# A macaron block (FFN, gated delta-rule attention, FFN) on one core: a new order of the attention core's products, statistics and halves, and centring on TensorE

## What is computed

```python
x = x + 0.5 * ffn(layernorm(x))
x = x + attn(layernorm(x))
x = x + 0.5 * ffn(layernorm(x))        # the same weights as the first

def ffn(x):
    h = silu(x @ w1.T * w1_s) * (x @ w2.T * w2_s)     # 128 -> 512
    h = gelu(h @ h1.T * h1_s)                          # 512 -> 512, exact gelu
    h = gelu(h @ h2.T * h2_s)                          # 512 -> 512
    return h @ w3.T * w3_s                             # 512 -> 128

def attn(hs):                                          # 4 heads of 32
    q, k, v = (silu(dwconv4(hs @ W)) for W in (Wq, Wk, Wv))
    beta = sigmoid(hs @ Wb)
    o_d = delta_rule_chunkwise(q, k, v, beta)          # chunks of 32: T = inv(I + strict(kb k')), then a recurrence over 8 chunks
    paths = [fir3(v), fir15(v), fir64(v), o_d, v]      # five paths, 32 wide per head
    stats = mean, mean square, mean abs, norm of each path, each broadcast over 32 channels
    logits = gelu([hs, stats] @ gW1 + gb1) @ gW2 + gb2
    probs = softmax(logits / tau) * (1 - sum(eps)) + eps
    o = sum_p probs_p * paths_p
    return (o * rsqrt(mean(o*o) + 1e-5) * norm_w) @ Wo
```

## Time and profile before

| | |
|---|---|
| median of 3 runs | 507.91 us (507.79 to 508.33) |
| the profiled execution | 507.65 us |
| its span, first to last instruction | 505.9 us |
| TensorE / weight loads / VectorE / ScalarE / GpSimd busy | 397.9 / 293.3 / 314.0 / 290.1 / 9.9 us |
| mean granted TensorE clock | 0.858 |

### The profile page before, as it was taken

One profiled execution on the slowest core, in us unless ns is written; L12 is line 12 of the kernel. 1 busy time (PEld: TensorE's weight loads), 2 busy tenths in 40 slices (PEclk: granted clock), 3 DMA queues, 4 the chain that ended last, 5 costly groups with the idle time before them and its releaser, 6 DMA issues.

```text
span 505.9 us, 9754 instructions
## 1 busy us (share of the span) xinstructions
PE 397.9 (79%) x4162; PEld 293.3 (58%) x4162; DVE 314.0 (62%) x467; ACT 290.1 (57%) x415; POOL 9.9 (2%) x36
## 2 busy tenths in 40 slices
PE   5579999999889869779587816608673599989997
PEld 2446776678657559477477814303322448666785
DVE  2883579565037597999154774893358845676633
ACT  5866857895665754965326133211525448686973
POOL 3000000000000100000100000000000000000000
PEclk9779999999999956979957556858786979999999
DMA  8700008100000000024700000000000000001001
GB/s 280 246 1 1 3 1 264 29 3 0 2 0 0 2 3 3 0 64 128 224 12 6 4 1 1 0 1 0 0 0 1 1 1 1 1 2 43 3 1 41
DMA packets 13428, 17.38 MB, mean 34 GB/s; under 512 B 832, under 2 KB 9024, under 8 KB 13376
## 3 DMA queue, kind: packets, MB, share of 16 engines
q1 hardware_dynamic: 13232, 16.58, 10.6%
q10 hardware_dynamic: 144, 0.01, 0.0%
HBM read 15.55 MB, written 1.05 MB: 33 GB/s over the span
## 4 chain that ended last, share of the span: by engine, by line
PE 56%; DVE 20%; ACT 14%; issue 8%; DMA 2%; SPq 0%; DVEq 0%; ACTq 0%
PE ps_a L654 11%; PE ps_a L655 11%; PE ps_a L848 5%; PE ps_a L745 4%; PE ps_a L789 3%; ACT arena L569 3%; DVE arena L1123 2%; PE ps_d L811 2%; PE ps_a L801 2%; PE ps_a L811 2%; DVE acts L968 2%; PE ps_d L712 2%; PE ps_d L655 2%; PE ps_d L654 2%; PE ps_a L832 1%
## 5 line engine op out<-in xcount | busy, mean ns | idle before, releaser
L654 PE MATMUL ps_a<-acts,w_f 128*128 128x512 f32 x256 | 104.4, 408 | 1.3 <-DVE acts L968 1.0
L655 PE MATMUL ps_a<-acts,w_f 128*128 128x512 f32 x256 | 101.4, 396 | 0.0
L654 PEld LDWEIGHTS ps_a<-acts,w_f 128*128 128x128 f32 x256 | 49.2, 192 | 14.7 <-issue 1.4
L655 PEld LDWEIGHTS ps_a<-acts,w_f 128*128 128x128 f32 x256 | 49.1, 192 | 11.6 <-issue 1.4
L539 ACT ACTIVATE acts<-ps_a,vec 128x512 fp32r<-128x512 f32 x64 | 44.3, 692 | 0.0
L987 DVE TENSOR_TENSOR acts<-gbuf,acts 128x512 fp32r<-128x512 f32 x32 | 21.6, 688 | 32.7 <-ACT acts L539 32.7
L745 PE MATMUL ps_a<-xnp,conv_w 128*128 128x512 f32 x156 | 38.3, 403 | 0.0
L987 DVE TENSOR_TENSOR acts<-ghbuf,acts 128x512 fp32r<-128x512 f32 x32 | 21.4, 690 | 25.4 <-ACT acts L539 25.4
L745 PEld LDWEIGHTS ps_a<-xnp,conv_w 128*128 128x128 f32 x156 | 29.3, 188 | 8.3 <-issue 1.4
L848 PE MATMUL ps_a<-arena,ident 128*128 128x512 f32 x40 | 22.8, 737 | 13.4 <-DVE arena L1123 13.4
L823 PE MATMUL ps_d<-arena 32*32 32x64 f32 x448 | 13.8, 275 | 24.4 <-issue 14.7
(11 more groups left out here) (192 smaller groups left out, 810.5 us busy)
## 6 DMA issues: line engine op xcount, KB each, us to landing
toep<-in_fir SPq DMA_DIRECT2D x16, 288.0 KB, 5.1
w_in<-in_h SPq DMA_DIRECT2D x4, 1024.0 KB, 8.4
g_rows<-in_gW SPq DMA_DIRECT2D x4, 640.0 KB, 6.6
w_in<-in_w SPq DMA_DIRECT2D x6, 256.0 KB, 4.1
iobuf<-in_x SPq DMA_DIRECT2D x4, 256.0 KB, 6.6
toep<-in_taps SPq DMA_DIRECT2D x1, 768.0 KB, 6.8
y<-iobuf SPq DMA_DIRECT2D x3, 256.0 KB, 2.4
toep<-in_proj SPq DMA_DIRECT2D x1, 256.0 KB, 9.0
```

The source lines that it names most:

```text
L654: e.matmul(bank, w, hi, start=start, stop=False)
L655: return e.matmul(bank, w, lo, start=False, stop=stop)
```

## The change

Nothing of the arithmetic's meaning changes. What is done, part by part:

- Layer norm: a third constant matrix `cent_w`, identity minus 1/128, so that the product of "mean" is x already centred, in PSUM. ScalarE squares it from there; VectorE's subtraction goes, and `refine` reads the centred x from PSUM. The bank is held until `refine` has read it.
- First FFN: "scan" of h1 stands before "var", "scan" of h2 and w3 behind the means of tiles 2 and 3, "flag" of it behind their "var". "flag" uses ring A and its number is made by ScalarE. The rounding of h2 and w3 stands behind the first "hid1" on ScalarE.
- Tables of ScalarE's functions are loaded ahead by one-element operations (`preload`).
- "gram": ScalarE copies one half out of each bank, VectorE masks the other. The temperature numbers on ScalarE so come behind gram.
- The last four "fir" groups are interleaved with "yy" of half 0. All statistics of paths 0 to 2 and 4 (both halves) are split into single reductions ("r1", "r2", "r3") and squares ("sq") and stand before and between the steps of half 0's recurrence. Half 1's recurrence has gates, logits and softmax of half 0 between its steps. "bo" of half 1 comes behind that recurrence of half 0, "aq" between its steps.
- "logit" leaves PSUM through ScalarE, with bias and scale.
- "mix" is in quarters ("mul" 0 to 3, 16 of the 32 tokens of each row each). Quarter 0 is added by identity products, the other three by three VectorE adds each ("add"), with a square on ScalarE ("osq").
- Gates 2 and 3 and logits 2 and 3 move into the second FFN around the first "up"; what is left of half 1 is put between single blocks of "hid1" and "hid2" by the table `FILL`, on VectorE and ScalarE. "wo" 2 and 3 come behind "hid2" of tile 0; mean and variance of tiles 2 and 3 behind "hid2" of tile 1.

```diff
@@ ffn_steps
-    s += [("soft", 2, 1)] if last else []
-    s += [("var", f, 0)]
-    s += [] if last else [("flag", f, 0)]
-    s += [("var", f, 1)]
+    s += [] if last else [("flag", f, 0), ("scan", f, 1)]
+    s += [("var", f, 0), ("var", f, 1)]
...
-            s += [("scan", f, 1), ("up", f, a), ("flag", f, 1), ("scan", f, 2), ("up", f, b), ("flag", f, 2)]
+            s += [("up", f, a), ("flag", f, 1), ("up", f, b)]
         elif more:
-            s += [("up", f, a), ("mix", 2, 1), ("up", f, b), ("addmix", 2, 1)]
+            s += [("gate", 2, 2), ("gate", 2, 3), ("up", f, a), ("logit", 2, 2), ("logit", 2, 3), ("up", f, b)]
...
-            s += [("hid1", f, a), ("scale", 2, 1), ("hid1", f, b), ("wo", 2, 2), ("wo", 2, 3), ("hid2", f, a),
-                  ("mean", f, 2), ("mean", f, 3), ("var", f, 2), ("var", f, 3), ("hid2", f, b)]
+            s += [("hid1", f, a), ("hid1", f, b), ("hid2", f, a), ("wo", 2, 2), ("wo", 2, 3), ("hid2", f, b),
+                  ("mean", f, 2), ("mean", f, 3), ("var", f, 2), ("var", f, 3)]
         elif more:
             s += [("hid1", f, a), ("in", f, a + 2), ("in", f, b + 2), ("mean", f, a + 2), ("mean", f, b + 2),
-                  ("hid1", f, b), ("var", f, a + 2), ("var", f, b + 2), ("hid2", f, a), ("hid2", f, b)]
+                  ("scan", f, 2), ("hid1", f, b), ("var", f, a + 2), ("var", f, b + 2), ("flag", f, 2), ("hid2", f, a), ("hid2", f, b)]
@@ att_steps
-    s += [("fir", 2, i) for i in range(16)]
-    s += [("turn4", 2, 0), ("turn4", 2, 1)]
-    s += [("yy", 2, h) for h in range(4)] + [("aq", 2, b) for b in range(4)]
-    s += [("stat", 2, 0)] + [("bo", 2, b) for b in range(4)] + [("round", 2, 0)]
-    ahead = [(kind, 2, 4 + k) for kind in ("yy", "aq", "bo") for k in range(4)]
-    extra = {2: ("stat", 2, 1), 4: ("stat", 2, 2), 6: ("stat", 2, 3), 7: ("stat", 2, 4)}
+    s += [("fir", 2, i) for i in range(12)]
+    for k in range(4):
+        s += [("yy", 2, k), ("fir", 2, 12 + k)]
+    s += [("turn4", 2, 0), ("turn4", 2, 1), ("sq", 2, 0), ("sq", 2, 1)] + sums(0) + [("sq", 2, 2)] + sums(1)
+    s += [("sq", 2, 3), ("aq", 2, 0), ("r1", 2, 2), ("aq", 2, 1), ("r2", 2, 2), ("r3", 2, 2), ("sq", 2, 4),
+          ("aq", 2, 2), ("r1", 2, 3), ("aq", 2, 3), ("r2", 2, 3), ("r3", 2, 3)]
+    s += [("bo", 2, b) for b in range(4)] + [("sq", 2, 5)] + sums(4)
+    ahead = [("yy", 2, k) for k in range(4, 8)] + [("aq", 2, k) for k in range(4, 8)]
+    between = {1: [("r1", 2, 5)], 2: [("r2", 2, 5), ("r3", 2, 5), ("sq", 2, 6)], 3: [("numbers", 2, 0), ("r1", 2, 6)],
+               4: [("r2", 2, 6), ("r3", 2, 6), ("sq", 2, 7), ("round", 2, 0)], 5: [("r1", 2, 7)], 6: [("r2", 2, 7)],
+               7: [("r3", 2, 7)]}
     for n in range(1, NCH):
-        s += [("rec", 2, n)] + ahead[2 * n - 2:2 * n]
-        s += [extra[n]] if n in extra else []
-    s += [("turn3", 2, 0), ("stat", 2, 5), ("turn", 2, 0)]
...
+        s += [("rec", 2, n), ahead[n - 1]] + between[n]
+    s += [("aq", 2, 7), ("turn3", 2, 0), ("sq", 2, 8)] + [("bo", 2, b) for b in range(4, 8)] + sums(8) + [("turn", 2, 0)]
+    half = [("rec", 2, NCH + n) for n in range(1, NCH)]
+    s += [half[0], ("gate", 2, 0), half[1], ("gate", 2, 1), half[2], ("logit", 2, 0), half[3], ("logit", 2, 1), half[4],
+          ("lturn", 2, 0), half[5], ("soft", 2, 0), half[6], ("prob", 2, 0), ("mul", 2, 0), ("addmix", 2, 0),
+          ("mul", 2, 1), ("add", 2, 1), ("osq", 2, 1), ("turn3", 2, 1), ("sq", 2, 9), ("rms", 2, 0), ("r1", 2, 9),
+          ("scale", 2, 0), ("r2", 2, 9), ("r3", 2, 9), ("wo", 2, 0), ("wo", 2, 1), ("turn", 2, 1)]
...
+FILL = {("hid1", 0, 0): [("lturn", 1)], ("hid1", 0, 1): [("soft", 1)], ("hid1", 0, 2): [("prob", 1)],
+        ("hid1", 0, 3): [("mul", 2)], ("hid1", 1, 1): [("mul", 3)], ("hid1", 1, 3): [("add", 2), ("osq", 2)],
+        ("hid2", 0, 0): [("add", 3), ("osq", 3)], ("hid2", 0, 2): [("rms", 1)], ("hid2", 0, 3): [("scale", 1)]}
@@ ScalarE
+            def preload(table):
+                settle()
+                own(e.activation(vc("rt0"), vc("lneps"), table))
+            def late(kind, i):
+                if kind == "soft":
+                    e.wait_ge(S["dve_sub"], i + 1)
+                    e.activation(ex5[:, i], ex5[:, i], ACT.Exp).then_inc(S["act_exp"], 1)
+                    preload(ACT.Gelu if i else ACT.Abs_reciprocal_sqrt)
+                elif kind == "osq":
+                    r = slice(HB * (i % 2), HB * (i % 2) + HB)
+                    e.wait_ge(S["summed"], i if i else 1)
+                    e.activation(o_sq[:, r], paths[0][:, i // 2, r], ACT.Square).then_inc(S["act_osq"], 1)
+                elif kind == "rms":
+                    e.wait_ge(S["dve_ms"], i + 1)
+                    e.activation(rt, var, ACT.Abs_reciprocal_sqrt).then_inc(S["act_rms"], 1)
+                    preload(ACT.Gelu if i else ACT.Sqrt)
...
+                elif kind == "flag":
+                    e.wait_ge(S["pe_a"], a + 1)
+                    e.activation(low_any[:, i:i + 1], bank[:, 0:1], ACT.Copy, scale=128.0).then_inc(S["act_a"], 1)
+                elif kind == "gram":
+                    e.wait_ge(S["dve_nrm"], NT)
+                    for h in range(H):
+                        e.wait_ge(S["pe_d"], dd + h + 1)
+                        e.activation(alt[:, i, h, :, 0], ps_d[:, (dd + h) % NRING].rearrange(
+                            "p (n a t) -> p n a t", n=NCH, a=2)[:, :, 0], ACT.Copy).then_inc(S["act_l"], 1)
...
+                        for k, n in FILL.get((kind, i, m), ()) if f else ():
+                            late(k, n)
+                    if s == ("hid1", 0, 0):
+                        e.wait_ge(S["ld_hid"], 32)
+                        e.activation(w_f[0][:, 3072:5632], w_in[0][:, 3072:5632], ACT.Copy).then_inc(S["hid_round"], 1)
@@ TensorE
-                    e.wait_ge(S["dve_d"], D_AT[("flag", 0, n)] + 1)
+                    e.wait_ge(S["act_a"], A_AT[("flag", 0, n)] + 1)
...
-                    e.matmul(take_d(dd), mean_w[:, :], tile(x_t, i), start=True, stop=True
+                    e.matmul(take_d(dd), cent_w[:, :], tile(x_t, i), start=True, stop=True
@@ VectorE
-            def refine(bank, half_y2, y, src, eps, out, shape, free):
-                e.scalar_tensor_tensor(out=half_y2, in0=bank, scalar=eps, in1=half_y2, op0=ALU.add, op1=ALU.mult
-                                       ).then_inc(S["dve_d"], 1)
-                own(e.scalar_tensor_tensor(out=src, in0=src, scalar=-1.0, in1=y, op0=ALU.mult, op1=ALU.mult))
+            def refine(bank, half_y2, y, centred, src, eps, out, shape, done, freed):
+                own(e.scalar_tensor_tensor(out=half_y2, in0=bank, scalar=eps, in1=half_y2, op0=ALU.add, op1=ALU.mult))
+                e.scalar_tensor_tensor(out=src, in0=centred, scalar=-1.0, in1=y, op0=ALU.mult, op1=ALU.mult
+                                       ).then_inc(S["dve_d"], done)
...
+                elif kind == "mul":
+                    g, r = i // 2, slice(HB * (i % 2), HB * (i % 2) + HB)
+                    w = pr5[:, g, r].rearrange("p t c -> p c t").unsqueeze(3).to_broadcast([128, P, HB, DH])
...
+                elif kind == "add":
+                    g, r = i // 2, slice(HB * (i % 2), HB * (i % 2) + HB)
+                    settle()
+                    own(e.tensor_tensor(pall[:, 0:2, g, r], pall[:, 0:2, g, r], pall[:, 2:4, g, r], ALU.add))
+                    settle()
+                    own(e.tensor_tensor(paths[0][:, g, r], paths[0][:, g, r], paths[1][:, g, r], ALU.add))
+                    settle()
+                    e.tensor_tensor(paths[0][:, g, r], paths[0][:, g, r], paths[4][:, g, r], ALU.add
+                                    ).then_inc(S["summed"], 1)
```

More of the change, by code:

```diff
@@ L99 @@
-RING_D = {"mean": 1, "flag": 1, "var": 1, "up": KT, "down": 1, "sumsq": 2, "gram": H, "aq": 1, "rec": 1,
-          "logit": 1, "wo": 1}
+RING_A = {"in": 1, "flag": 1, "gsum": 1, "up": KT, "hid1": KT, "hid2": KT, "out": 1, "qkv": 4, "window": 1, "token": 1, "fir": 1,
+          "yy": 1, "bo": 1, "gate": 2, "logit": 1, "addmix": 1}
+RING_D = {"mean": 1, "var": 1, "up": KT, "down": 1, "sumsq": 2, "gram": H, "aq": 1, "rec": 1,
+          "wo": 1}
 def ring_of(step):
```

299 lines of the change are left out of this document (151 added, 148 removed).

## The result

The changed kernel takes 484.27 us (median of 4 runs, 483.71 to 485.25); the kernel before, run beside it, 507.85 (506.75 to 508.33). The ratio is 0.9541, 95% interval 0.9519 to 0.9563: 23.6 us faster. The forecast was 487.5, in a range of 473 to 500. The profiled execution of the changed kernel has a span of 483.5 in 485.25 us.

What follows compares the result with a forecast made beforehand. TensorE was busy 79% of the span, but the bound was taken to change from stage to stage. 507.65 us with +4.4 -0.25 -25.1 +0.8 = -20.2 gave 487.5; own range 480 to 494, 8 in 10 473 to 500.

Steps and rivals of the forecast that it cites:

- 1. First FFN: First FFN: removed waits give -8.2 us; rounding, the flag ahead of hid2 and clock falls turn it to +4.4.
- 2. Convolution to inverse: Convolution, gram, inverse: +0.3 us; centring spares 0.25, gram evacuation costs 0.5, the temperature numbers nothing at the end.
- 3. To the first state: Up to half 0's recurrence: +2.6 us including gram's 0.5; VectorE's queue moves the first state's transpose from 265.1 to 267.7.
- 4. Recurrences: Both halves' recurrences: -8.4 us at half 1's first state (VectorE 26.2 plus waits), then -32.8 at the output projection.
- 5. Second FFN's start: Softmax, multiply and addmix leave, gates and logits enter: hid1 at 363.3 instead of 416.1, -52.8 us there.
- 6. What is given back: Second FFN: half 1's work between hidden blocks gives back 27.7 us; TensorE waits 20 for "wo 2"; -25.1 is left.
- The pause looked for ahead of "out": Second FFN, a sign of being right: TensorE idle about 5 us before "out", followed by a granted clock of 0.5.
- The fillers don't fit: Rival, second FFN: fillers fit, TensorE finds wo 2 ready, 16 of the 20 us come back, 471; chance 0.10.
- The flag isn't free: Rival, first FFN: the flag costs nothing, hid1's pauses are covered, -8.2 stays instead of +4.4, 475; chance 0.15.
- The core gives: Rival, half 0: core doesn't give, instruction supply or slow clock bounds it, -8.4 and 3 more go, 499; chance 0.15.
- The clock doesn't stay low: Rival, hid2 of tile 1 to the end: clock stays low after the 20-us pause, up to 537; chance 0.05.

Runs made afterwards that it cites:

- flag_first: Changed kernel with the h2 flag moved ahead of the variances of tiles 2 and 3 in the first FFN: 478.78 us, ratio 0.9432.
- no_centre: Changed kernel with the mean product and VectorE's subtraction brought back, no centring on TensorE: 488.82 us, ratio 0.9646.
- numbers_first: Changed kernel with ScalarE's temperature numbers back in front of gram: 484.38 us, ratio 0.9528.
- short_abs: Changed kernel whose VectorE sums of absolute values read only 4 of the 32 channels of a head: 483.46 us, ratio 0.9513.
- wo_late_lag: Changed kernel with "wo" 2 and 3 behind hid2 of tile 1, and ScalarE's squares and root one or two gelus later: 475.56 us, ratio 0.9374.

## Why the prediction held, step by step

Positions before and after (us into the span), with the shift that the steps of the prediction give, sums of its steps, and the shift measured:

| position | before | after | forecast | measured |
|---|---|---|---|---|
| attention core starts | 124.14 | 127.91 | +4.4 | +3.8 |
| first state, half 0 | 265.12 | 269.59 | +6.8 | +4.5 |
| first state, half 1 | 306.49 | 300.74 | -4.3 | -5.8 |
| "wo 0" | 370.32 | 341.27 | -28.7 | -29.1 |
| hid1, second FFN | 416.06 | 365.71 | -48.7 | -50.4 |
| hid2 of tile 1 | 445.75 | 414.71 | -29.7 | -31.0 |
| first silu, tiles 2 and 3 | 460.70 | 438.31 | -21.0 | -22.4 |
| end of the span | 505.9 | 483.5 | -20.2 | -22.4 |

(Forecast shifts of the rows from half 0 on are the steps' figures plus 4.4 - 0.25.)

**1. First FFN.** Right in kind and near in size. hid1 starts at 26.94, 5.9 earlier (5.3 forecast), and its first tile runs at full clock, worth 2.9 as forecast. (Its instructions there are 32, not 64; the 7.3 us of the prediction fit 32.) The pause ahead of the means takes back 4.0 (2.9 forecast) and the fall of the clock behind it 1.9 (2.4): from 40.27 to the end of hid1 at 51.30 are 11.0 us, from 45.05 to 54.17 they were 9.1. hid2 starts 2.1 later than before (56.06 to 58.17), where +2.0 was forecast, and the second fall of the clock costs 1.7 by the core's start, not 2.4. flag_first shows that the flag is the cause of the second pause.

**2. Convolution to inverse.** By VectorE's last operation of the norms 1.6 of the 3.8 are gone again (187.58 to 189.79), where 0.25 was forecast for centring. no_centre is 1.9 late where the core starts and 2.4 at gram (189.43 against 187.02), so some 0.6 of this is centring. Another 0.5 is a shorter run of VectorE's `refine` for tile 2 (4.6 us from 166.28 before, 4.1 from 169.28 after, and 4.1 in no_centre too); the rest is open. The handing over of gram costs the 0.5 forecast (188.19 to 190.93, +2.7). That the temperature numbers cost nothing fits numbers_first.

**3. To the first state.** VectorE has no idle time from 252.6 to 269.6, as expected, and needs 17.0 for what was put at 17.5. But it starts at 252.56, not at 254.4 (250.2 with steps 1 and 2 on top): FIR moved only 0.9 against gram (3.6 less 2.7), where 1.9 was forecast for the numbers ahead of it. The hole of TensorE under the weight loads fell into the first "bo", not into "aq"; as forecast, VectorE's queue covered it.

**4. Recurrences.** The gains are of the size forecast (-11.0 from the first state of half 0 to that of half 1, measured -10.2; -24.4 from there to "wo 0", measured -23.3). (The prediction's own positions, 298.3 and 306.5, give -8.2, not the -8.4 of its heading; nothing else rests on it.) The reason given for the first was incomplete: "On VectorE half 0 is ... 26.2 us" reads as if VectorE were the bound and waits came on top. short_abs took 3.7 us out of that sum (four reductions, 0.93 each) and the turn of the statistics came no earlier (299.33 against 298.96). The round through TensorE and then ScalarE's line of square, load, copies and root are as long. The number came out because waits of near that size were in the sum: 4.4 us forecast, 5.3 measured (1.23 and 0.37 at the first two steps, 1.52 and 0.46 at "aq", 1.73 before the turn). The claim of one bound was wrong, and that it did the number no harm is luck.

**5. Second FFN's start.** -20.0 from "wo 0" to hid1, measured -21.3.

**6. What is given back.** Forecast 20 us of idle TensorE ahead of "wo 2" at 408.4; measured 19.70 at 410.93. From the hid2 layer of tile 1 to the first silu 8.7 are lost against before by the forecast, 8.6 by the trace, though with a mechanism that was not foreseen: the next "down" doesn't follow "var" but waits 2.62 for `refine`, since the banks of mean and variance are held until then, in a ring that "down" needs. VectorE's row at its release:

```profile
427.87 0.69 DVE L958 SCALAR_TENSOR_TENSOR arena<-ps_d,arena 128x512 f32<-128x512 f32 x1 [3.08 <-ACT arena L532]
428.48 0.68 DVE L959 SCALAR_TENSOR_TENSOR arena<-ps_d,arena 128x512 f32<-128x512 f32 x1
```

ScalarE's waits for the sums were forecast and came (7.57, 3.35 and 0.80), but up to 394.67 they hold VectorE up nowhere (wo_late_lag), so that they are at most a part of why "wo 2" is late. The pause looked for ahead of "out", about 5 us, is this one of 2.62 ahead of "down"; the clock is 0.50 from 431 to 433.

**The rivals.** The fillers don't fit (19.70 of idle time). The flag isn't free (flag_first: 5.5). The core gives. The clock doesn't stay low: 0.50 from 400 to 412, 0.83 from 412 to 424, 1.00 in the last 48 us. In the profiled executions the forecast is 2.2 us above the measured end: 0.6 from step 1, 1.7 from steps 2 and 3, -0.8 and -1.1 from the two halves of step 4, 1.3 from step 5, -0.3 in the first part of step 6, and 0.8 for a clock that cost nothing more. Errors of both signs stand in this sum; that it is as near as 2.2 is in part luck. The other 1.0 to the median is that the profiled execution after is itself 1.0 above its median.

## What to carry to other kernels

When an engine chooses a branch by a number that another engine makes, put the making of that number ahead of any longer work in that engine's queue: here a one-element copy behind two variances cost 5.5 us. When the last consumer of a long side chain stands in the middle of the bounding engine's stream, place it behind independent work (8 us for one swapped pair). And before crediting one engine with a stage, take work off that engine alone: if its time comes back as waits, the bound is shared.
